# A tile loop turned into a ring of 16 steps, with each hop between engines in a step of its own

## The chip, the cores and the metric

The kernel runs on one core of a Trainium2 chip. The metric is the device time of one launch in microseconds (us); lower is better. A core has five engines that work side by side, each from an instruction stream of its own, in order: TensorE (PE, matmuls and transposes into PSUM banks; PEld is its weight load), VectorE (DVE), ScalarE (ACT), GpSimd (POOL) and SyncE (SP, which here only starts DMAs). They meet at semaphores. An instruction that waits holds up all that stands behind it on its engine.

## The reference, cut to what matters

1024 tokens of 256 features (32 sequences of 32) go through three residual blocks:

```python
x = x + xattn(layernorm(x), ctx)   # 16 heads, 257 context rows of 64 per sequence, low-rank weights
x = x + attn(layernorm(x))         # 16 heads of 128, self-attention within 32 tokens, mxfp4 weights and biases
x = x + ffn(layernorm(x))          # router over 64 experts, top 8, capacity 128; silu(gate) * up, down
```

In the third block a token's slot in an expert is its rank among the tokens that chose that expert, counted over the tokens in order; tokens past slot 127 are dropped.

## The kernel before, in words

The tokens are cut into T = 8 tiles of 128 (four sequences each). The program has three stages: the weights of the first block are multiplied together ("fold"), then the tile loop, then the 64 experts.

In the tile loop each tile passes two pipelines. The first (X, tile i) is the cross-attention: 16 rows (4 sequences times 4 groups of heads). A row is `score_row` on PE (L1188, L1189), `max_row` on DVE (L830), `exp_row` on ACT (L609), `transpose_row` on PE (L1196), `copy_row` on ACT (L617) and `sum_row` on PE (L1207); every four rows DVE's `normalise` (L836 to L840) ends a sequence. Beside the rows stand the units of the list `XS`: `kt0` to `kt3` (the keys of a sequence, L1166, split in a high part by ACT and a low part by DVE, L592, L820), `cT0` to `cT3` (L1171), and, for the next tile, `hT` (L1155), `qa` and `qb` (the queries of 8 head pairs, L1161, L588, L824); `out` is the output product (L1175) that DVE's `x_out` adds to the tokens (L847). The second pipeline (S, tile j = i - 1, with parts for m = j - 1) is the self-attention and the routing, the list `SS`: `hT`, `q0` to `q3`, `k0` to `k3` (L1142 to L1144, drained by DVE in L867), `sc` (L1234, softmax L872 to L859), `v0` to `v3` (drained by ACT, L630), `pv0` to `pv3` (L1244, split by ACT L634 and DVE L883); and for tile m `wo0` to `wo3`, `rT`, `log`, `pos` with DVE's `self_out` (L928), `chosen` (L903 to L907), `weigh`, `place` (L919 to L921). Both lists go through two PSUM banks each, a unit to one bank in turn, so unit n can start only when unit n - 2 has been drained. DVE's `norm_root` and `norm_apply` (end L811) make the layernorms; `next_h1` (L946) makes the one of the next tile.

The order of work is written out by hand. Every engine runs the same function `tile(i, j, m)` of STEPS = 21 steps: steps 0 to 15 each hold one row, and the tables `X_AT` and `BEHIND` say at which step a unit stands, on all engines. Rows and the units of X come ahead of the units of S in a step. The last five steps have no score row: `qb` stands at step 18, `cT3` and `kt0` at 19, `out` at 20, and only then does the next call of `tile` begin, whose row 0 waits for `qb` and `kt0`. A unit's matmuls, its drain by ACT and its drain by DVE are all in the same step.

POOL makes the rotated context (`rope_products` L456 to L461, `rope_sums` L471), the last of the 257 rows (`last_rows` L479), the low parts of the weights in tile 0 (L503), and scatters the rows of tile m to the experts with 8 indirect DMAs (`scatter`, L488) once `slot` is known; `scattered` then frees `h3`. SP's queue loads the context of tile i when the sums of tile i - 1 are made. The S pipeline starts with tile 0 when the X pipeline is at tile 1; after the last tile come two calls without X. The experts start when the last scatter has landed.

Of the kernel before, what the change touches and what calls it, by code (L numbers as in the profile page):

```python
# [12 lines left out]
P = 128  # L13
# [17 lines left out]
XS = ["kt1", "kt2", "cT0", "kt3", "cT1", "cT2", "hT", "qa", "qb", "cT3", "kt0", "out"]  # L31
XSPLIT = ["kt1", "kt2", "kt3", "qa", "qb", "kt0"]
XNEXT = ("hT", "qa", "qb", "kt0")
# [4 lines left out]
SS = ["wo", "hT", "q0", "q1", "q2", "q3", "k0", "rT", "k1", "k2", "log", "k3", "sc", "v0", "pos", "v1", "v2", "v3",  # L38
# [28 lines left out]
def build(nc, x, ctx_in, Wq, kcq, kckv, Wqr, Wkr, Wo_x, codes, scales, bq, bk, bv, bo, rw, gup, dnp,  # L67
# [5 lines left out]
    with ctx:  # L73
# [189 lines left out]
        def xpos(name, i, more=1):  # L263
            n, i = XS.index(name), i if name in XNEXT else i + 1
            return n % 2, i * (len(XS) // 2) + n // 2 + more

# [7 lines left out]
        def high_count(name, i):  # L274
            return (i if name in XNEXT else i + 1) * len(XSPLIT) + XSPLIT.index(name) + 1

# [148 lines left out]
        def _(e):  # L425
# [24 lines left out]
            def rope_products(i):  # L450

                if not isinstance(i, int) or i > 0:
                    e.wait_ge(roped, i * (2 * BT))
# [29 lines left out]
            def scatter(j):  # L483

                e.wait_ge(slot_ready, j + 1)
                alone(e)
                for k in range(TOPK):
                    e.indirect_dma_start(XE[:, :], bass.IndirectOffsetOnAxis(ap=slot[:, k:k + 1], axis=0), h3[:, :], None,  # L488
                                         bounds_check=E * CAP - 1, oob_is_err=False).then_inc(scat, 16)
# [18 lines left out]
            def tile(i, m, last=False):  # L508
                if not last:
                    rope_products(i + 1)  # L510
                for b in range(BT):
                    last_rows(i, b)
                    if isinstance(i, int) and i == 0:
                        for r, u in TILE_PARTS.items():
                            if RB * b <= r < RB * (b + 1):
                                part_low(u)
                    if b == BT - 1 and m is not None:
                        scatter(m)
                    if not last:
                        rope_sums(i + 1, b)  # L520
                if m is not None:
                    scattered(m)

            tile(0, None)

            e.wait_ge(w_done, PARTS)
            e.memset(diag[:, :, :], 0.0).then_inc(zeroed, 1)
            tile(1, None)

            e.wait_ge(zero_out, 16 * (E // 8 + NY))  # L530
            for j in range(1, T - 2):
                tile(j + 1, j - 1)
            tile(T - 1, T - 3, last=True)
            for m in (T - 2, T - 1):
                scatter(m)
                scattered(m)
# [17 lines left out]
        def _(e):  # L554
# [44 lines left out]
            def exp_row(i, r):  # L599
                e.wait_ge(maxed, i * ROWS + r + 1)  # L600
                if r % RB == 0:

                    b = r // RB
                    if b >= 2:
                        e.wait_ge(on_ready, i * BT + b - 1)
                    elif not isinstance(i, int) or i > 0:
                        e.wait_ge(on_ready, i * BT + (b - 1))
# [4 lines left out]
            def copy_row(i, r):  # L612
                e.wait_ge(transposed, i * ROWS + r + 1)

                if r >= 2:
                    e.wait_ge(summed, i * ROWS + r - 1)
# [27 lines left out]
            def spread(j, q):  # L644

                e.wait_ge(sT_ready, j + 1)
# [3 lines left out]
            def tile(i, j, m, last=False):  # L650


                def uses(names):
                    for name in names:
                        t = m if name in BEFORE else j
                        if t is not None:
                            s_use(name, t)

                for r in range(STEPS):
                    if i is not None:  # L660
                        if 2 <= r <= ROWS + 1:
                            copy_row(i, r - 2)
                        if r < ROWS:
                            exp_row(i, r)
                        for name in X_AT.get(r, ()):
                            if name in XNEXT and not last:
                                x_use(name, i + 1)
                            elif name not in XNEXT and name != "out":
                                x_use(name, i)
                        if isinstance(i, int) and i == 0 and r in TILE_PARTS:  # L670
                            part_high(TILE_PARTS[r])
                    if j is not None and r in (13, 14):
                        for q in (0, 1) if r == 13 else (2, 3):
                            spread(j, q)
                    uses(BEHIND.get(r, ()))


            e.sem_inc(x_high, XSPLIT.index("qa"))
            for name in XNEXT:
                x_use(name, 0)  # L680

            tile(0, None, None)

            e.wait_ge(zeroed, 2)
            tile(1, 0, None)
            for j in range(1, T - 2):
                tile(j + 1, j, j - 1)
            tile(T - 1, T - 2, T - 3, last=True)
            tile(None, T - 1, T - 2)
            tile(None, None, T - 1)  # L690
# [19 lines left out]
        def _(e):  # L710
# [10 lines left out]
            def link(ins, which, base):  # L721

                done[which] = done.get(which, 0) + 1
                s, n = LINKS[which]
                ins.then_inc(s, 1)
                e.wait_ge(s, base * n + done[which])
# [20 lines left out]
            def all_stats(half):  # L747
# [8 lines left out]
                else:  # L756
                    e.wait_ge(n_link, 2 * T)
                    done["n"] = 2 * T
# [84 lines left out]
            def x_out(i):  # L843
# [5 lines left out]
                norm_stats(i, "s", i, st1, mv1)  # L849
# [89 lines left out]

            def self_out_norm(j):  # L940
# [9 lines left out]
            def tile(i, j, m, last=False):  # L950

                done.clear()

                def uses(names):
                    for name in names:
                        t = m if name in BEFORE else j
                        if t is not None and name[:2] != "wo":
                            s_use(name, t)

                for r in range(STEPS):  # L960
                    if i is not None:
                        if r < ROWS:
                            max_row(i, r)
                        if r % RB == 2 and r > RB:
                            normalise(i, r // RB - 1)
                        for name in X_AT.get(r, ()):
                            if name in XSPLIT and name not in XNEXT:
# [3 lines left out]
                        if r == 8 and not last:  # L971
                            next_h1(i + 1)
# [442 lines left out]
```

## Time and profile before

| | us |
|---|---|
| median of 3 runs | 780.78 |
| lowest, highest | 779.69, 794.77 |
| the profiled execution | 785.1 |
| its span | 783.3 |
| mean granted TensorE clock, share of full | 0.909 |

The profile is of one execution. Its span runs from the first to the last instruction; 1.8 us of the execution's time lie around it. Busy times are sums over instructions. A matmul's end is modelled, so after the last of a row of matmuls PE counts as busy for a moment more. A time in brackets in a timeline is how long the engine sat idle before the instruction, with what released it.

### The profile page before, as it was taken

To read this page: it belongs to the slowest core of one execution; us is meant where nothing else is said; L and a number is where in the kernel's file an instruction comes from. 1 tells how busy PE (TensorE), PEld (TensorE's weight loads), DVE (VectorE), ACT (ScalarE), POOL (GpSimd) and SP (SyncE) were. 2 spreads that over 40 slices of the span, in tenths; PEclk is the share of its full clock that TensorE was granted. 3 is DMA by queue.
4 is the path that set the end of the run, shared out by engine and by line. 5 is a ranking of instruction groups with operands and counts; after the bars stand their busy time and mean duration, and the time that the engine had idled before them with its cause. 6 is when DMAs were issued, how large, how long until landed. Compare 5 with 4: busy or idle time off the path is not lost.

```text
span 783.3 us, 16249 instructions
## 1 busy us (share of the span) xinstructions
PE 622.6 (79%) x6211; PEld 534.6 (68%) x6211; DVE 426.4 (54%) x1091; ACT 288.1 (37%) x798; POOL 294.7 (38%) x279
## 2 busy tenths in 40 slices
PE   6995677898999987898899798898874178898860
PEld 4884566797877876787787696796753067777750
DVE  1255485465676675676576577577653323333334
ACT  1123364337346345236236236246031033333320
POOL 3113299211214414313412412400303337777780
PEclk9975567999999999999999999999999579999995
DMA  7946993999001101100100200100101069999988
GB/s 200 293 140 156 237 251 84 294 338 300 6 2 53 38 3 54 35 3 34 55 3 18 72 2 2 69 2 2 66 2 51 28 167 284 301 301 296 303 168 275
DMA packets 98987, 97.61 MB, mean 125 GB/s; under 512 B 26238, under 2 KB 92848, under 8 KB 98912
## 3 DMA queue, kind: packets, MB, share of 16 engines
q1 hardware_dynamic: 86016, 78.21, 34.2%
q0 software_dynamic: 12288, 17.95, 10.5%
q8 instruction: 51, 0.84, 0.4%
q10 hardware_dynamic: 608, 0.42, 0.2%
q14 instruction: 24, 0.20, 0.1%
HBM read 62.32 MB, written 35.19 MB: 124 GB/s over the span
## 4 chain that ended last, share of the span: by engine, by line
PE 43%; DVE 20%; issue 13%; ACT 9%; POOL 6%; DMA 6%; another core or an unknown queue 2%; SPq 0%; POOLq 0%; DVEq 0%; PEldq 0%; ACTq 0%
POOL expert_sums L545 6%; PE bank L1161 5%; PE bank L1175 5%; PE bank L1142 5%; PE bank L1144 4%; PE bank L1143 4%; PE bank L1207 4%; DMA expert_sums<-Wh,etok 3%; PE bank L1244 3%; ACT pr L609 2%; DVE nmax L830 2%; PE bank L1196 2%; ACT diag L648 2%; ACT space L630 2%
## 5 line engine op out<-in xcount | busy, mean ns | idle before, releaser
L545 POOL DMA_INDIRECT expert_sums<-Wh,etok x64 | 98.8, 1544 | 37.8 <-issue 22.5
L609 ACT ACTIVATE pr<-bank,nmax 128x257 f32<-128x257 f32 x128 | 61.0, 477 | 101.4 <-DVE nmax L830 101.0
L1142 PE MATMUL bank<-space,Wh 128*128 128x128 f16 x512 | 88.3, 219 | 9.9 <-DVE X L928 7.1
L488 POOL DMA_INDIRECT expert_rows<-h,slot x64 | 62.7, 980 | 87.5 <-DVE slot L921 70.4
L1143 PE MATMUL bank<-space,Wh 128*128 128x128 f16 x512 | 88.2, 219 | 0.0
L1144 PE MATMUL bank<-space,Wl 128*128 128x128 f16 x512 | 88.2, 219 | 0.0
L1207 PE MATMUL bank<-Cr,pT 128*128 128x64 f32 x512 | 77.0, 276 | 9.4 <-DVE On L840 8.4
L471 POOL TENSOR_TENSOR Cr<-C,Ct 128x192 f32<-128x192 f32 x64 | 41.7, 675 | 104.9 <-PE bank L1207 104.8
L1207 PEld LDWEIGHTS bank<-Cr,pT 128*128 128x128 f32 x512 | 72.4, 204 | 12.4 <-issue 11.1
L830 DVE TENSOR_REDUCE nmax<-bank 128x1 f32<-128x257 f32 x128 | 53.3, 418 | 42.8 <-PE bank L1189 40.6
L479 POOL TENSOR_TENSOR On<-Cr,pr 128x256 f32<-128x256 f32 x32 | 20.7, 647 | 138.4 <-ACT pr L609 138.4
L1345 PE MATMUL bank<-Wh,ring 128*96 128x128 f32 x512 | 68.1, 277 | 0.0
L617 ACT COPY pT<-bank 128x256 f32<-128x256 f32 x128 | 47.6, 372 | 43.0 <-PE bank L1196 42.3
L1142 PE MATMUL bank<-Wh,space 128*128 128x256 f16 (+1 forms) x192 | 59.2, 309 | 4.8 <-ACT space L630 3.3
L867 DVE SCALAR_TENSOR_TENSOR space<-bank,bqk 128x512 f32<-128x512 f32 x64 | 43.5, 689 | 33.1 <-PE bank L1144 33.0
L1345 PEld LDWEIGHTS bank<-Wh,ring 128*96 128x96 f32 x512 | 60.9, 166 | 0.4 <-issue 0.3
L1196 PE MATMUL bank<-ident,pr 128*128 128x128 f32 x256 | 52.6, 289 | 10.5 <-ACT pT L617 10.5
L1142 PEld LDWEIGHTS bank<-space,Wh 128*128 128x128 f16 x512 | 51.1, 100 | 13.0 <-DVE X L928 8.2
L1143 PE MATMUL bank<-Wl,space 128*128 128x256 f16 (+1 forms) x192 | 59.1, 308 | 0.0
L1144 PE MATMUL bank<-Wh,space 128*128 128x256 f16 (+1 forms) x192 | 59.1, 308 | 0.0
L1354 PE MATMUL bank<-ring,Wh 96*128 96x256 f32 x128 | 43.4, 420 | 13.4 <-DVE Wh L1031 9.9
L1143 PEld LDWEIGHTS bank<-space,Wh 128*128 128x128 f16 x512 | 50.1, 98 | 0.1
(175 smaller groups left out, 1401.0 us busy)
## 6 DMA issues: line engine op xcount, KB each, us to landing
ring<-L_ffn_gate_up_proj_dram SPq DMA_DIRECT2D x64, 192.0 KB
expert_rows<-h SPq DMA_DIRECT2D x8, 1284.0 KB, 15.7
Wh<-expert_rows SPq DMA_DIRECT2D x64, 160.5 KB
ring<-L_ffn_down_proj_dram SPq DMA_DIRECT2D x64, 96.0 KB
expert_sums<-h SPq DMA_DIRECT2D x4, 1152.0 KB, 13.4
C<-ctx_dram SPq DMA_DIRECT2D x24, 128.0 KB, 3.3
Wl<-expert_sums SPq DMA_DIRECT2D x3, 1024.0 KB, 6.9
space<-L_xattn_Wo_dram SPq DMA_DIRECT2D x8, 256.0 KB, 4.8
```

The costliest lines, as they stand in the source:

```text
L488: e.indirect_dma_start(XE[:, :], bass.IndirectOffsetOnAxis(ap=slot[:, k:k + 1], axis=0), h3[:, :], None, bounds_check=E * CAP - 1, oob_is_ ...
L545: e.indirect_dma_start(Y[n % NY][:, :], bass.IndirectOffsetOnAxis(ap=etok[:, n % 4:n % 4 + 1], axis=0), ye[:, n % 4], None, bounds_check=Y ...
L609: e.activation(pr[:, s, :], bank[r % 2][:, 0:NL], ACT.Exp, bias=nmax[:, s:s + 1], accum_out=rsum[:, s:s + 1]).then_inc(expd, 1)
L617: e.copy(pT[:, r % 2], bank[2][:, 0:2 * P].rearrange("p (c t) -> p c t", c=2)).then_inc(pt_ready, 1)
L830: e.tensor_reduce(nmax[:, s:s + 1], bank[r % 2][:, 0:NL], AX.X, ALU.max, negate=True).then_inc(maxed, 1)
L867: e.scalar_tensor_tensor((qS, kS)[w][:, 4 * g:4 * g + 4, :], src[:, :].rearrange("p (h t) -> p h t", h=4), 1.0 / WS, bqk[:, w, 4 * g:4 * g ...
L1142: e.matmul(dst, ah, bh, start=first and n == 0, stop=False)
L1143: e.matmul(dst, ah, bl, start=False, stop=False)
L1144: ins = e.matmul(dst, al, bh, start=False, stop=last and n == len(terms) - 1)
L1196: ins = e.transpose(bank[2][:, c * P:(c + 1) * P], pr[:, r % (2 * RB), c * P:(c + 1) * P], ident[:, :])
L1207: ins = e.matmul(bank[3][:, o:o + DC], pT[:, r % 2, c, :], Cr[:, b, c, 0, :], start=c == 0, stop=c == 1)
L1345: ins = e.matmul(bank[2 + n % 2][0:I, half * P:(half + 1) * P], gu[:, n, c, half * I:(half + 1) * I], xeT[:, n % 2, c, :], start=c == 0, s ...
```

## The change

All engines now run one ring: `step(g, t)` for n = 16 g + t, without a pause between tiles. A tile's rows stand at steps 0 to 15 of turn g, its last transposes and sums at steps 0 to 2 of the next turn, `cT3` at step 3, `out` at step 4; the S pipeline of a tile begins at step 5 and ends at step 3 of the turn after that. ACT and DVE have tables of their own, in which the drain by ACT and the drain by DVE often stand a step after the matmuls. Row 0 waits only for `qa`, row 2 for `qb`. DVE's `chosen` and `weigh` move behind the softmax, `pos` behind `v2`. POOL's work is put at steps, and the scatter is made in four pairs at steps 3 to 6.

```diff
-XS = ["kt1", "kt2", "cT0", "kt3", "cT1", "cT2", "hT", "qa", "qb", "cT3", "kt0", "out"]
+XS = ["kt1", "cT3", "out", "kt2", "cT0", "kt3", "cT1", "hT", "kt0", "qa", "qb", "cT2"]
+XTILE = {"cT3": -1, "out": -1, "hT": 1, "kt0": 1, "qa": 1, "qb": 1}
-X_AT = {2: ["kt1"], 6: ["kt2"], 7: ["cT0"], 10: ["kt3"], 11: ["cT1"], 15: ["cT2", "hT"], 16: ["qa"], 18: ["qb"],
-        19: ["cT3", "kt0"], 20: ["out"]}
+X_AT = {2: ["kt1"], 3: ["cT3"], 4: ["out"], 6: ["kt2"], 7: ["cT0"], 10: ["kt3"], 11: ["cT1"], 12: ["hT", "kt0"],
+        13: ["qa"], 15: ["qb", "cT2"]}
+X_LOW_AT = {3: ["kt1"], 7: ["kt2"], 11: ["kt3"], 13: ["kt0"], 14: ["qa"], 16: ["qb"]}
-BEHIND = {0: ["wo0"], 1: ["wo1"], 2: ["wo2"], 3: ["hT", "wo3"], 4: ["q0"], 5: ["q1"], 6: ["q2", "q3"], 7: ["k0", "rT"],
-          8: ["k1", "k2", "log"], 9: ["k3"], 10: ["sc"], 11: ["v0", "pos"], 12: ["v1"], 13: ["v2"], 14: ["v3"],
-          15: ["pv0"], 16: ["pv1"], 17: ["pv2"], 18: ["pv3"]}
+S_FIRST = 5
+S_AT = {5: ["wo0", "wo1"], 6: ["wo2"], 7: ["hT", "wo3"], 8: ["q0", "q1"], 9: ["q2", "q3"], 10: ["k0"],
+        11: ["rT", "k1", "k2"], 12: ["log", "k3"], 13: ["sc"], 14: ["v0"], 15: ["v1"], 0: ["v2"], 1: ["pos", "v3"],
+        2: ["pv0", "pv1"], 3: ["pv2", "pv3"]}
+ACT_S_AT = {7: ["hT"], 11: ["rT"], 13: ["log"], 14: ["sc", "v0"], 15: ["v1"], 0: ["v2"], 1: ["v3"], 2: ["pv0", "pv1"],
+            3: ["pv2", "pv3"]}
+DVE_S_AT = {7: ["hT"], 8: ["q0", "q1"], 9: ["q2", "q3"], 10: ["k0"], 11: ["k1", "k2"], 12: ["log", "k3"], 13: ["sc"],
+            1: ["pos"], 3: ["pv0", "pv1"], 4: ["pv2", "pv3"]}
-STEPS = ROWS + 5
+ALL_STEPS = ROWS * (T + 2) + 9
...
+            def step(g, t):
+                if t == 0 and 1 <= g <= T:
+                    last_rows(g - 1, 3)
+                if t == 3 and 1 <= g < T:
+                    rope_sums(g, 3)
+                if t == 4 and g < T:
+                    last_rows(g, 0)
+                if t in (3, 4, 5, 6) and 3 <= g < T + 3:
...
+                    scatter(g - 3, (2 * t - 6, 2 * t - 5))
+                if t == 6 and g + 1 < T:
+                    rope_products(g + 1)
+                if t in (7, 11, 15) and g + 1 < T:
+                    rope_sums(g + 1, t // 4 - 1)
+                if t in (8, 12) and g < T:
+                    last_rows(g, t // 4 - 1)
+                if t == 8 and 3 <= g < T + 3:
+                    scattered(g - 3)
...
+            def step(g, t):
+                n = ROWS * g + t
+                j, m = turn_of(g, t)
+                if j is not None and t == 5:
+                    x_out(j)
+                if g < T:
+                    max_row(g, t)
+                if t % RB == 2 and RB + 2 <= n and n - RB - 2 < T * ROWS:
+                    normalise(*divmod((n - RB - 2) // RB, BT))
...
+                if j is not None and t == 5:
+                    norm_stats(j, "s", j, st1, mv1)
+                    norm_root("s", j, mv1, rs1)
+                if j is not None and t == 6:
+                    norm_apply(h2, j, "s", j, mv1, rs1, h2_ready)
+                if m is not None and t == 8:
+                    self_out(m)
+                if m is not None and t == 9:
+                    norm_root("r", m, mv2, rs2)
+                if m is not None and t == 10:
...
+                    self_out_norm(m)
...
+                if j is not None and t == 15:
+                    softmax_sum(j)
+                    softmax_end(j)
+                if m is not None and t == 0:
+                    chosen(m)
+                if m is not None and t == 1:
+                    weigh(m)
+                if m is not None and t == 2:
+                    place(m)
+                if t == 11 and g + 1 < T:
+                    next_h1(g + 1)
...
-                if r == 0:
-                    wait_pos(e, xd, xpos("qb", i))
+                if r in (0, 2):
+                    wait_pos(e, xd, xpos("qb" if r else "qa", i))
...
-                    e.wait_ge(on_ready, i * BT + b)
+                    e.wait_ge(x_link, 2 * (i * BT + b) - 1)
```

The first `step` is POOL's, the second DVE's; in DVE's the units of `DVE_S_AT` stand between `self_out_norm` and `softmax_sum`. ACT's has `copy_row`, `exp_row`, the units of `X_AT`, two of the four `spread` (L648, the softmax laid out as diagonal blocks) at steps 0 and 1 each, then the units of `ACT_S_AT`. PE's has `score_row`, the transposes of the row two steps back, the sums of the row three back, the units of `X_AT`, then those of `S_AT`. The last hunk lets the sums of a new sequence start after the first of `normalise`'s three instructions, not the third.

## Rows read from the trace of the kernel before

**Rows 1.** The span in 40 slices of 19.6 us, in tenths.

```profile
PE   6995677898999987898899798898874178898860
...
PEclk9975567999999999999999999999999579999995
```

**Rows 2.** Busy time by stretches: us; PE, PEld, DVE, ACT, POOL busy; clock; DMA; GB/s.

```profile
145.60:200.60 55.00, 51.32 (x627) 45.43 (x626) 32.33 (x74) 26.26 (x75) 12.82 (x18) 1.00 0.91 294
200.60:258.00 57.40, 52.90 (x646) 46.77 (x644) 38.91 (x104) 27.42 (x79) 17.24 (x21) 1.00 0.07 25
258.00:318.20 60.20, 52.33 (x621) 45.21 (x620) 39.55 (x104) 27.14 (x79) 19.01 (x23) 0.97 0.12 35
...
379.70:441.20 61.50, 53.64 (x634) 46.78 (x632) 40.54 (x103) 27.22 (x79) 19.08 (x23) 0.97 0.09 30
...
503.30:555.00 51.70, 46.90 (x593) 41.16 (x591) 34.33 (x97) 24.53 (x73) 7.59 (x10) 1.00 0.04 14
...
555.00:631.40 76.40, 36.42 (x490) 29.21 (x487) 33.31 (x97) 10.09 (x22) 18.29 (x19) 0.82 0.11 36
```

**Rows 3.** Waits of PE from 379.7 to 441.2 us: total, times, longest.

```profile
PE bank L1166 <- DVE qspace L824: 2.5, 1, 2.5
PE bank L1207 <- DVE On L840: 1.3, 1, 1.3
PE bank L1142 <- DVE X L928: 1.3, 1, 1.3
PE bank L1220 <- DVE h L811: 1.1, 1, 1.1
PE bank L1175 <- ACT cT L597: 0.7, 1, 0.7
```

**Rows 4.** Timeline of PE: start, us, instruction, idle before.

```profile
251.92 0.55 PE L1166 MATMUL bank<-ident,Cr 128*128 128x128 f32 x3 [1.57 <-DVE qspace L824]
252.32 3.69 PE L1175 MATMUL bank<-N,cT 128*128 128x256 f32 x16
...
415.86 0.27 PE L1188 MATMUL bank<-KTh,qspace 128*128 128x257 f16 x1
...
417.99 0.27 PE L1188 MATMUL bank<-KTh,qspace 128*128 128x257 f16 x1
...
433.98 0.55 PE L1166 MATMUL bank<-ident,Cr 128*128 128x128 f32 x3 [2.49 <-DVE qspace L824]
435.25 5.38 PE L1175 MATMUL bank<-N,cT 128*128 128x256 f32 x16 [0.72 <-ACT cT L597]
```

**Rows 5.** Groups of DVE from 379.7 to 441.2 us: busy us, mean ns, idle before.

```profile
L830 DVE TENSOR_REDUCE nmax<-bank 128x1 f32<-128x257 f32 x17 | 7.1, 418 | 9.4 <-PE bank L1189 9.1
...
L824 DVE TENSOR_TENSOR qspace<-bank,qspace 64x512 f16<-64x512 f32 x4 | 2.8, 689 | 2.7 <-issue 1.9 <-ACT qspace L588 0.8
...
L907 DVE TENSOR_REDUCE mask<-space 128x64 bf16<-128x512 f32 x1 | 1.1, 1096 | 0.0
```

**Rows 6.** Groups of ACT in the same stretch.

```profile
L609 ACT ACTIVATE pr<-bank,nmax 128x257 f32<-128x257 f32 x16 | 7.6, 476 | 15.7 <-DVE nmax L830 15.6
...
L648 ACT COPY diag<-space 32x512 f32<-32x512 f32 x4 | 2.4, 612 | 0.1
L630 ACT ACTIVATE space<-bank 128x512 f32<-128x512 f32 x4 | 2.4, 602 | 0.3 <-PE bank L1144 0.3
```

**Rows 7.** Timeline of DVE after the last output product: one undisturbed layernorm.

```profile
554.98 0.42 DVE L847 TENSOR_TENSOR X<-X,bank 128x256 f32<-128x256 f32 x1 [4.24 <-issue]
...
558.59 0.41 DVE L811 TENSOR_SCALAR h<-X,mv,rs 128x256 f32<-128x256 f32 x1
```

**Rows 8.** The scatter's group of POOL from 379.7 to 441.2 us.

```profile
L488 POOL DMA_INDIRECT expert_rows<-h,slot x8 | 7.8, 978 | 5.6 <-DVE slot L921 3.5 <-issue 2.1
```

**Rows 9.** Timelines of DVE and of POOL at 323 us.

```profile
323.05 1.97 DVE L811 TENSOR_SCALAR h<-X,mv,rs 128x256 f32<-128x256 f32 x1
...
323.07 1.80 POOL L461 TENSOR_TENSOR C<-C,cosT 128x768 f32<-128x768 f32 x1
```

More of the change, by code:

```diff
@@ L506, in _ @@
                 part_low(u)
[L508 to L536, printed above, removed]
+            def step(g, t):
[6 more added lines that the diff above has]
+                if t in (3, 4, 5, 6) and 3 <= g < T + 3:
+                    if g == 3 and t == 3:
+                        e.wait_ge(zero_out, 16 * (E // 8 + NY))
+                    scatter(g - 3, (2 * t - 6, 2 * t - 5))
[7 more added lines that the diff above has]
+                    scattered(g - 3)
+                if g == 0 and t in TILE_PARTS:
+                    part_low(TILE_PARTS[t])
+                if g == 1 and t == 9:
+                    e.wait_ge(w_done, PARTS)
+                    e.memset(diag[:, :, :], 0.0).then_inc(zeroed, 1)
+            for n in range(ALL_STEPS):
+                step(n // ROWS, n % ROWS)
             def add_out(j, first):
@@ L648, in spread @@
                 e.copy(diag[qs, :, qs], sT[qs]).then_inc(diag_ready, 1)
[L650 to L675, printed above, removed]
@@ L678, in _ @@
[L678 to L690, printed above, removed]
+            def step(g, t):
+                row = row_of(ROWS * g + t - 2)
+                if row:
+                    copy_row(*row)
+                if g < T:
+                    exp_row(g, t)
+                for name in X_AT.get(t, ()):
+                    if name != "out" and 0 <= g + XTILE.get(name, 0) < T:
+                        x_use(name, g + XTILE.get(name, 0))
+                if g == 0 and t in TILE_PARTS:
+                    part_high(TILE_PARTS[t])
+                j, m = turn_of(g, t)
+                if j is not None and t in (0, 1):
+                    spread(j, 2 * t)
+                    spread(j, 2 * t + 1)
+                for name in ACT_S_AT.get(t, ()):
+                    if name in BEFORE and m is not None:
+                        s_use(name, m)
+                    elif name not in BEFORE and j is not None:
+                        s_use(name, j)
@@ L692, in expert_copy @@
+            e.sem_inc(x_high, XSPLIT.index("kt0"))
+            for name in XS:
+                if XTILE.get(name, 0) == 1:
+                    x_use(name, 0)
+            for n in range(ALL_STEPS):
+                step(n // ROWS, n % ROWS)
             def expert_copy(ex, n):
@@ L1011, in _ @@
             next_h1(0)
-            for name in ("qa", "qb", "kt0"):
-                x_low(name, 0)
-            tile(0, None, None)
-            tile(1, 0, None)
-            e.wait_ge(zero_out, 16 * (E // 8 + NY))
-            e.tensor_scalar(h3[:, D + E:ROW], h3[:, D + E:ROW], float(-(B * S + P)), None, ALU.add).then_inc(zeroed, 1)
-            e.wait_ge(zeroed, 3)
-            for j in range(1, T - 2):
-                tile(j + 1, j, j - 1)
-            tile(T - 1, T - 2, T - 3, last=True)
-            tile(None, T - 1, T - 2)
-            tile(None, None, T - 1)
+            for name in XSPLIT:
+                if XTILE.get(name, 0) == 1:
+                    x_low(name, 0)
+            for n in range(ALL_STEPS):
+                step(n // ROWS, n % ROWS)
+            assert all(done[which, i] == count for which, count in (("x", XLINKS), ("s", SLINKS), ("r", RLINKS))
+                       for i in range(T)), done
             def experts(j, first):
@@ L1333, in expert_t @@
+            for name in XS:
+                x_item(name, -1)
+            for n in range(ALL_STEPS):
+                step(n // ROWS, n % ROWS)
             def expert_t(j, n):
```

188 lines of the change are left out of this document (83 added, 105 removed).

## The prediction, made before the change was run

> **What bounds the kernel now.** I first read the page: the PE and clock lines in slices [rows 1]. Up to 145 us the clock sits at about half and the weights of the fold and of the second block stream in. From 145 to 555 us (slices 7 to 27) PE is nearly full at the full clock. Then come a thin stretch to 631 us and the experts, which this change leaves alone. So the place to look is the tile loop, and the question is what PE lacks there.
>
> Second, busy time cut at the moments when DVE adds the cross-attention's product (`x_out`, L847) [rows 2]. The seven stretches are 55.0, 57.4, 60.2, 61.5, 61.5, 62.1 and 51.7 us. In a full one (379.7 to 441.2) PE is busy 53.6 of 61.5 us, DVE 40.5, ACT 27.2, POOL 19.1, and the clock is 0.97. PE is the bound engine, with 7.9 us of idle time.
>
> Third, PE's waits in that stretch [rows 3]: 2.5 for the low part of `qb` and 0.7 for `cT` at the seam, 1.3 for `normalise`, 1.3 for `self_out`, 1.1 for the layernorm, 6.9 of the 7.9. Fourth, the seam itself [rows 4]: PE stops 2.49 us before `kt0`, then 0.72 us, and the 16 matmuls of `out` take 5.38 us. Three tiles earlier, behind a stop of 1.57, they took 3.69. That is the clock's lower level (1.2 in place of 2.4 GHz) after the stop, worth 1.7 us. It happens in four of the seven stretches. A tile without any stop would take 61.5 - 7.9 - 1.7 = 51.9 us.
>
> **The seam goes.** Removed per full tile: the stops of 2.5 and 0.7 and the 1.7 of the clock, 4.9 us. `qb` is now needed only by row 2 of the next turn, and its drain has steps 15 and 16; `kt0` stands at step 12, three steps ahead of its use; `out` at step 4 has rows, `wo0` and `wo1` around it. The stop of `normalise` (1.3) goes too: the sums of a sequence wait for its first instruction, ahead of the two others. That makes 6.2. The stops of 1.3 and 1.1 stay in kind, since `self_out` and `hT` still are one hop each; they are in the next part.
>
> **What is late next.** I lay out one turn. Beyond its units every PE step has a row. One row and one `v` unit take 2.13 us (415.86 to 417.99) [rows 4]; the mean step is 51.9 / 16 = 3.2 us. A DVE instruction of 512 columns takes 0.69 us, `max_row` 0.42, the mask 1.10 [rows 5]. An `exp_row` holds ACT 0.48 us and a further read of its accumulator, some 0.57 in all; a `spread` takes 0.61 and a `v` copy 0.60 [rows 6]. The stops of the new turn:
>
> - `pos` at step 1, the largest. It needs DVE's mask. From the end of `sc` DVE has, in order: two softmax steps (1.4), a max and `normalise` (1.5), the low part of `qa` (1.3), a max and the softmax's end (2.8), a max and the low part of `qb` (1.8), and `chosen` (0.2 + 0.7 + 1.1): 10.8 us. PE has in that time the rows of steps 14 to 1, `v0` to `v2`, `qb` and `cT2`: three times 2.13, one more row of 0.8 and about 2.1 for the rest, 9.3 us. Stop: 1.5. Before, `chosen` stood with `k3`, where DVE had time.
> - `pv2` at step 3. It needs the drain of `pv0`, which on DVE stands behind `place` (1.6, step 2) and the low part of `kt1`: 1.0.
> - `hT` of S at step 7: from `x_out` to the layernorm's end DVE needs 4.0 us with nothing between (554.98 to 559.00) [rows 7], here with two maxes and one `normalise` (2.1) and a wait for step 6, 7.1 in all; PE has 7.0 us of work in steps 5 to 7. Stop: 0.2.
> - `q0` at step 8, behind `self_out`: 0.4 (1.3 before: it stood behind more of DVE's waits for ACT).
> - `rT`, `k1`, `k2` at step 11: they wait for `self_out_norm`, for the drain of `k0` behind it, and for `rT`'s copy behind `exp_row`: 0.3, 0.4, 0.2.
> - `hT` of X at step 12: `next_h1` stands last in DVE's step 11, behind the drain of `k2`: 0.4.
> - `pv0` at step 2: ACT's copy of `v3` stands behind two of the `spread`: 0.25.
>
> Together 4.65. In the profile's counting each stop is 0.16 shorter, since PE counts as busy for 0.16 after its last matmul, so nine stops come to 3.2.
>
> **POOL and DVE together.** One mechanism speaks against the new places. At 323.05 `norm_apply`'s last instruction took 1.97 us, where it takes 0.41 alone [rows 7, 9]; it ended as POOL's L461 (1.80 us, from 323.07) did. DVE's instruction waited while POOL worked on SBUF. Before, this hit two of the full tiles. Now the eight scatters (0.98 each, 1.3 apart with the issue gaps [rows 8]) stand ahead of `rope_products` on POOL: from the slots at step 3 they run about 10.3 us, with `last_rows` between, so the products (L461 and two shorter instructions) fall on steps 5 to 7, where `normalise` and `norm_apply` stand and `hT` has no slack. I take 0.7 us a tile. The bounds: 0, when they miss each other, and 2.0, when both DVE instructions meet L461 for its 1.80 us. The Trainium skill's page GPSIMD Engine Reference, section Key points, says that GpSimd shares its SBUF interfaces with VectorE and contends with instructions in a 2-port mode or with two SBUF inputs. By that rule alone (L811 and L840 both fall under it) a collision would be the rule in every tile rather than in two, and the sum would carry the 2.0; the trace agrees on the kind, with its 1.97 against 0.41.
>
> For short stops that I can't see I add 0.7 (the three smallest of the tile now come to 7.9 - 6.9 = 1.0). A full turn: 51.9 + 3.2 + 0.7 + 0.7 = 56.5 us. Bounds of what the trace can't show, the sum of the new stops: 0 and, if each of `pos` and `pv2` waits 2 us longer and the clock falls once (1.7), 3.2 + 4 + 1.7 = 8.9, so 51.9 to 62.2 a turn. I take 56.5, since each of its terms is a sum of measured durations.
>
> **The sum.** Three turns against 61.5, 61.5 and 62.1: 5.0 + 5.0 + 5.6 = 15.6. The one against 60.2: 3.7. Against 57.4 (no clock loss there): 56.0, so 1.4. Against 55.0 (no part for tile m, so no `pos`): 53.0, so 2.0. The last, against 51.7 with 46.9 busy: 49.5, since fewer units cover the same hops, so 2.2. Up to the first `x_out` five rows of tile 1 are now done as well, in a stretch that the loads of the weights hold (DMA is behind it, not PE): 1.5 earlier, between 0 and 4. After the last `x_out` 76.4 us pass to the experts [rows 2], a chain of single hops with PE 36.4 busy. Its order is nearly the same; `chosen` leaves the way of the softmax (2.0) but `pos` now holds `v3`: 1.0 earlier, between 2 later and 3 earlier. The scatter in pairs costs nothing: POOL works 19.1 of 61.5 us, the last pair's end is behind by less than a step, and `scattered` at step 8 stands two steps ahead of its need (`h3` at step 10). In the last two turns POOL has nothing else. The expert stage is unchanged.
>
> Total 15.6 + 3.7 + 1.4 + 2.0 + 2.2 + 1.5 + 1.0 = 27.4. The profiled execution's 785.1 becomes 757.7 (span 755.9). The median of the runs shown stands 4.3 below the profiled execution; 780.8 - 27.4 gives **753** for the median.
>
> **The rivals.**
> - *The ring closes fully.* The stops I worked out overlap with each other (a delay at `pos` gives DVE time for `place`), and a turn takes near 51.9. Against the seven stretches: 9.6 + 9.6 + 10.2 + 8.3 + 5.5 + 3.7 + 4.8 = 51.7, with the two ends 54: 727. For it: DVE has 21 us free in a tile. Against: DVE's free time doesn't lie between `sc` and `pv`, where it is busy for some 17 us in a row. Chance 0.10.
> - *The seam moves.* The stop at `pos` grows beyond 2.4, so that the clock falls there as it did at 433.98. A turn: 56.5 + 1.5 + 1.7 = 59.7, which gives back 3.2 in five turns, 16 us: 769. For it: one slow link in DVE's long chain is enough, as `normalise` with POOL beside it. Against: a stop of 1.57 leaves `out` at 3.69 [rows 4], and `pos` has 1.5. Chance 0.18.
> - *Slower.* DVE's chain from `sc` to `pv3` becomes the ring. The mechanism is `place`, `chosen` and `pos` between the maxes: `max_row` of steps 1 to 3 comes late, so `exp_row`, so the scores two rows on, and `pv` as well. It decides once DVE's stretch from step 13 to 4 is over 5 us longer than I have it: then both stops pass 2.5 us, and the clock falls twice: 56.5 + 5 + 3.4 = 64.9, 3.4 to 7.5 worse than before in five turns (21 us in all), less some 3 of the 6.7 won at the ends: 798. Chance 0.07.
> - *The change doesn't do what it says*: `out` or row 0 still wait a whole hop at the turn (`cT3` is copied by ACT behind `exp_row` of step 3). Its cover is `pv2`, `pv3` and a row, over 2.5 us against 2.0. If it fails, 0.7 to 2 us a turn: about 760, inside my range, and I count it in.
>
> **How the numbers follow.** 0.65 for 753 (its own range 744 to 764, from turns of 55 to 58.5), 0.10 for 727, 0.18 for 769, 0.07 for 798. The range 737 to 773 leaves out the last and most of the first. Faster by over 2% means below 765.2 (2% is about what a measurement of this kernel can tell from no change): nearly all of the first case, the ring closing, and a little of the moved seam: 0.76. Within 2%: the rest of those, 0.17. Slower by over 2%: 0.07.
>
> **What would show it.** Stretches between `x_out`s of 55.5 to 57.5 us at a clock of 1.00, `out` at about 3.7 us in all of them, and no wait of PE for `qspace` L824 or `cT`. A wait of L1258 (`pos`) for the mask of 1 to 2 us, and one of L1244 for DVE L883 of about 1, each once a turn. POOL's L461 beside a long L811 or L840. Wrong would be: a clock of 0.97 in the full turns, a wait over 2.4 us at `pos`, DVE idle of less than 10 us a turn, or a stretch behind the last `x_out` that differs from 76 by more than 3.

## The result and the profile after

| | before | changed |
|---|---|---|
| median, us (20 runs each) | 786.51 | 780.06 |
| lowest, highest | 779.69, 795.37 | 765.58, 789.67 |
| the profiled execution | 785.1 | 783.59 |
| its span | 783.3 | 781.8 |
| mean granted clock | 0.909 | 0.894 |
| first `x_out` | 145.63 | 149.67 |
| last `x_out` | 554.98 | 553.24 |

The change makes the kernel 1.4% faster here: the ratio is 0.9858, with a 95% interval of 0.9815 to 0.9900. (On the second chip of the experiments no difference can be told: 0.9959, with 0.9868 to 1.0049.) The ratio compares undisturbed runs alone, so it isn't the quotient of the two medians. The forecast, 753 us within 737 to 773, was wrong: 27.4 us were promised, and some 6.5 (by the medians) to 11 (by the ratio) came.

The page after, the span in 40 slices of 19.5 us (those of before are [rows 1]):

```profile
PE   6999577898998899898988989899875088888850
...
PEclk9955657899999999999999999999998579999995
```

The tile loop still fills slices 7 to 27 and the clock line still reads 9, so the page doesn't tell why. The stretches between the `x_out`s do (L848 now; columns as in [rows 2]; the cut at 552.80 stands 0.4 us ahead of the last `x_out`, so the seventh stretch is really 48.0 us):

```profile
149.70:206.90 57.20, 52.32 (x627) 45.84 (x626) 31.84 (x72) 26.63 (x75) 15.66 (x19) 0.97 0.94 292
206.90:263.30 56.40, 51.60 (x634) 45.67 (x633) 39.71 (x103) 27.29 (x79) 12.67 (x18) 1.00 0.07 20
263.30:323.30 60.00, 53.40 (x634) 46.94 (x633) 40.50 (x102) 27.55 (x79) 18.85 (x24) 0.97 0.09 30
323.30:383.90 60.60, 54.79 (x634) 48.31 (x633) 40.56 (x102) 27.45 (x79) 18.71 (x23) 0.94 0.09 30
383.90:443.80 59.90, 53.40 (x635) 46.40 (x633) 40.31 (x102) 27.55 (x79) 18.72 (x23) 0.97 0.09 30
443.80:505.20 61.40, 54.82 (x634) 47.16 (x633) 40.42 (x102) 27.54 (x79) 18.68 (x23) 0.94 0.06 23
505.20:552.80 47.60, 44.35 (x567) 38.65 (x566) 32.62 (x90) 20.67 (x59) 9.08 (x10) 1.00 0.07 26
552.80:631.00 78.20, 40.03 (x506) 32.11 (x506) 33.66 (x97) 12.25 (x26) 19.42 (x20) 0.80 0.15 50
```

Two columns matter. The clock: the turn at 1.00 takes 56.4 us, where 56.0 was forecast; the four behind it have 0.97 or 0.94 and take about 60 to 61. PE's busy time: the same 634 instructions need 51.60 us at 1.00, 53.40 at 0.97 and 54.8 at 0.94, so one step of the clock column is 1.4 to 1.8 us. PE works longer on the same work; its idle time, 5.8 to 6.6 us in these four turns, is less than the 7.9 of before.

PE's waits in the turn from 323.3 to 383.9 (total, times, longest):

```profile
PE bank L1251 <- DVE mask L907: 1.9, 1, 1.9
PE bank L1213 <- DVE h L812: 1.7, 2, 1.2
PE bank L1163 <- DVE On L841: 1.1, 1, 1.1
PE bank L1237 <- DVE space L883: 0.6, 1, 0.6
PE bank L1147 <- DVE h L952: 0.4, 1, 0.4
```

Against [rows 3], the stops for `qspace` and for ACT's `cT` are gone, and nothing waits at the turn. The new first is `pos` (L1251, the mask), the second S's `hT` (L1213), the third one that I hadn't: a `cT` unit (L1163) that waits for `normalise`.

Where the clock falls is seen in short windows behind these stops, two behind the pair of L1163 and L1213 and two behind `pos`:

```profile
331.00:340.00 9.00, 7.58 (x77) 6.72 (x78) 5.33 (x17) 1.94 (x7) 1.70 (x3) 0.81 0.00 0
391.00:400.00 9.00, 6.82 (x87) 6.34 (x88) 6.57 (x19) 2.31 (x8) 2.13 (x4) 1.00 0.01 2
...
250.00:256.00 6.00, 5.59 (x45) 4.59 (x45) 5.36 (x16) 4.92 (x13) 1.14 (x2) 1.00 0.12 26
...
369.00:377.00 8.00, 7.16 (x45) 6.07 (x45) 6.41 (x18) 5.30 (x14) 1.19 (x3) 0.79 0.15 35
```

Each kind of stop appears once with the clock fallen (0.81, 0.79) and once without (1.00). Over the whole loop the clock fell behind two of the four pairs and behind four of the five stops at `pos`. It fell a seventh time in the first stretch, behind a pause of PE that the kernel before didn't have, in the middle of the small matmuls of the first `sc`; the profile names nothing that PE waited for there:

```profile
182.31 0.33 PE L1227 MATMUL bank<-space 128*32 128x32 f32 x16 [2.33 <-issue]
```

The timeline of PE shows one of each kind of stop (start, us, instruction, idle before):

```profile
331.23 0.41 PE L1163 MATMUL bank<-ident,On 128*128 128x128 f32 x2 [1.14 <-DVE On L841]
332.83 0.41 PE L1213 MATMUL bank<-ident,h 128*128 128x128 f32 x2 [1.20 <-DVE h L812]
...
333.30 0.27 PE L1136 MATMUL bank<-Wh,space 128*128 128x256 f16 x1
...
334.21 0.42 PE L1135 MATMUL bank<-Wl,space 128*128 128x256 f16 x1
...
336.13 0.91 PE L1200 MATMUL bank<-Cr,pT 128*128 128x64 f32 x4
...
369.75 0.19 PE L1251 MATMUL bank<-mask,before 128*128 128x64 bf16 x1 [1.91 <-DVE mask L907]
...
372.04 0.95 PE L1200 MATMUL bank<-Cr,pT 128*128 128x64 f32 x4
...
376.12 0.56 PE L1200 MATMUL bank<-Cr,pT 128*128 128x64 f32 x4
...
380.24 3.67 PE L1167 MATMUL bank<-N,cT 128*128 128x256 f32 x16
```

The same form of four sums takes 0.91 or 0.95 us behind a stop and 0.56 later, and a 256-column matmul 0.42 for 0.27: the lower level, 1.2 GHz. `out`, which took 5.38 at the seam [rows 4], takes 3.67. The fall has not gone with the seam; it has moved, and mostly to two places.

The third stop has its cause on POOL. Timelines of DVE and of POOL at 329 us:

```profile
328.37 0.42 DVE L831 TENSOR_REDUCE nmax<-bank 128x1 f32<-128x257 f32 x1 [2.44 <-PE bank L1182]
...
329.37 1.71 DVE L841 TENSOR_TENSOR On<-On,rinv 128x256 f32<-128x256 f32 x1
...
332.27 0.41 DVE L812 TENSOR_SCALAR h<-X,mv,rs 128x256 f32<-128x256 f32 x1
```

```profile
328.99 1.81 POOL L481 TENSOR_TENSOR C<-C,cosT 128x768 f32<-128x768 f32 x1
```

`normalise`'s last instruction took 1.71 us, alone 0.43, and ended 0.28 us after the last instruction of POOL's `rope_products`. This is the collision that the prediction named, on L841 and not on L812. The first row is a second finding: DVE sat idle for 2.44 us, waiting for the score of row 6, with the end of S's layernorm queued behind.

Outside the loop: from the last `x_out` to the end 228.6 us, before 228.3. The first `x_out` came 4.0 us later, though the tile work in front of it is not slower: `next_h1` of tile 0, which ends the fold, whose code is unchanged, starts 5.8 us later than before. In ten profiles of nearly the same front this first `x_out` lies anywhere between 137.0 and 149.7 us, and this is why the loop below is compared from the first to the last `x_out`: before 409.3, changed 403.6.

### The profile page after: what moved, and what is told of

It reads as the page before. It is cut to its first block, busy times and chain, and to the rows that moved or that the text cites. A ratio compares the mean times of both kernels' runs of the same rounds, so it can differ in the third digit from the quotient of the medians.

```text
span 781.8 us, 16320 instructions
## 1 busy us (share of the span) xinstructions
PE 633.0 (81%) x6211; PEld 542.4 (69%) x6211; DVE 427.2 (55%) x1091; ACT 289.7 (37%) x798; POOL 293.8 (38%) x279
## 4 chain that ended last, share of the span: by engine, by line
PE 43%; DVE 25%; issue 12%; POOL 8%; DMA 6%; another core or an unknown queue 2%; ACT 2%; SPq 0%; POOLq 0%; DVEq 0%; PEldq 0%; ACTq 0%
PE bank L1134 5%; PE bank L1136 5%; PE bank L1135 5%; POOL expert_sums L563 5%; DMA expert_sums<-Wh,etok 4%; PE bank L1167 3%; PE bank L1237 3%; PE bank L1200 3%; PE bank L1153 3%; DVE On L841 3%; DVE qspace L825 2%; PE bank L1123 2%; PE bank L1111 2%; PE bank L1182 2%
## 5 line engine op out<-in xcount | busy, mean ns | idle before, releaser
L491 POOL TENSOR_TENSOR Cr<-C,Ct 128x192 f32<-128x192 f32 x64 | 38.5, 624 | 169.5 <-PE bank L1200 165.2
L1200 PEld LDWEIGHTS bank<-Cr,pT 128*128 128x128 f32 x512 | 75.1, 211 | 0.8 <-issue 0.5
L1134 PE MATMUL bank<-Wh,space 128*128 128x256 f16 (+1 forms) x192 | 61.8, 322 | 2.7 <-issue 2.4
L1136 PE MATMUL bank<-Wh,space 128*128 128x256 f16 (+1 forms) x192 | 62.1, 323 | 0.0
L1135 PE MATMUL bank<-Wl,space 128*128 128x256 f16 (+1 forms) x192 | 61.9, 323 | 0.0
L1134 PEld LDWEIGHTS bank<-space,Wh 128*128 128x128 f16 x512 | 50.8, 99 | 6.7 <-DVE space L867 2.8
L1034 DVE CAST etok<-Wh 128x1 uint32<-128x1 f32 x64 | 9.8, 153 | 73.9 <-DMA expert_sums<-Wh,etok 55.7
```

Of the source, the lines that this page charges most:

```text
L1134: e.matmul(dst, ah, bh, start=first and n == 0, stop=False)
L1135: e.matmul(dst, ah, bl, start=False, stop=False)
L1136: ins = e.matmul(dst, al, bh, start=False, stop=last and n == len(terms) - 1)
L1200: ins = e.matmul(bank[3][:, o:o + DC], pT[:, r % 2, c, :], Cr[:, b, c, 0, :], start=c == 0, stop=c == 1)
```

## The experiments

The theory after the first reading: the hand-laid stops stand about where they were put, and what is missing is the clock, which falls behind the stop at `pos` and behind the pair of `cT` and `hT`, plus POOL's collision in front of that pair; take the stops away and the falls go with them. The rivals: DVE's chain, or the scatter in pairs, sets the pace of the ring, and PE's stops only show it. A full turn is one of the third to sixth stretches. Stops of an experiment are named by the changed kernel's lines; where POOL's code has grown, lines behind it are six higher (L1213 is L1219, L1251 is L1257, L841 is L847, L883 is L889).

| kernel | median (runs) | ratio to before, 95% | loop, us | falls in it |
|---|---|---|---|---|
| before, first set | 786.44 (7) | | | |
| `chosen` ahead of `sc` | 770.2 (4) | 0.9822 (0.9761 to 0.9882) | 396.6 | 5 |
| products later | 767.55 (4) | 0.9751 (0.9700 to 0.9801) | 394.5 | 5 |
| both | 756.8 (4) | 0.9643 (0.9601 to 0.9685) | 383.1 | 0 |
| scatter in one block | 773.96 (4) | 0.9851 (0.9793 to 0.9909) | 397.5 | 2 |
| before, second set | 777.31 (19) | | | |
| before with the early sums | 783.16 (10) | 0.9959 (0.9887 to 1.0031) | 405.8 | 4 |
| both, layernorm first | 745.26 (4) | 0.9597 (0.9496 to 0.9698) | 373.7 | 0 |
| products later, `v3` ahead of `pos` | 755.66 (4) | 0.9731 (0.9657 to 0.9805) | 385.3 | 1 |
| the changed kernel again | 780.71 (10) | 0.9959 (0.9868 to 1.0049) | 407.9 | 8 |

The two sets ran on two chips, each with its own runs of before, so medians are compared within a set only; in the second, before spread from 762.0 to 793.3 us. The loop, from the first to the last `x_out`, and the falls of the clock in it are of one profile each; in the first profiles they were 409.3 us with 4 falls (before) and 403.6 with 7 (changed). On the second chip the changed kernel can't be told from before. Against the changed kernel's 0.9858 (0.9815 to 0.9900), the ratios of "products later" and "both" are clearly lower, that of `chosen` ahead of `sc` is not; there the profile has to tell.

**`chosen` ahead of `sc`.** DVE makes the mask at step 13, not at step 0 of the next turn; nothing else.

```diff
+                if m is not None and t == 13:
+                    chosen(m)
...
-                if m is not None and t == 0:
-                    chosen(m)
```

> The changed kernel with DVE's chosen at step 13, ahead of the softmax's maximum, where DVE sat idle for 2.5 us waiting for sc; pos keeps its place. Theory (two stops a turn, each with a fall of the clock behind it): the wait of pos for the mask (1.9 us) and the half-clock stretch behind it (3.6 us long, so about 1.8 us) go. A full turn falls from 60.6 to 57, the clock of the turns is 0.97, the kernel gains 3 to 3.5 us in each of 6 turns, about 18 us. Rival A (DVE is the bound of the ring from sc to pv3, wherever chosen stands): the stop moves to pv0 or pv2, the turn stays within 1 us of 60. Rival B (the clock falls whatever the stops are): the stop goes, the clock stays at 0.94 to 0.97, the turn is 58.7.

Measured: 770.2 us; full turns of 60.0, 58.5, 58.5 and 58.9. PE's waits from 309.0 to 367.5:

```profile
PE bank L1213 <- DVE h L812: 1.7, 2, 1.2
PE bank L1163 <- DVE On L841: 1.1, 1, 1.1
PE bank L1237 <- DVE space L883: 0.8, 1, 0.8
PE bank L1134 <- ACT space L643: 0.7, 1, 0.7
```

The stop at `pos` is gone, the pair stands, and the clock of the turn is 0.97, one step up from 0.94. In this profile it falls behind each of the four pairs and nowhere else in the full turns; in the turn of 60.0 it stayed down about twice as long (0.58 over 7.2 us). I had expected 57, with this one fall already in it, so the miss of one and a half us is idle time: between two turns that I compare (60.6 and 58.5 us) PE's idle time falls from 5.8 to 5.0 us, not by the whole 1.9, since a stop of 0.7 for ACT's drain of a `v` unit (L643) is new.

**Products later.** POOL's `rope_products` and the first `rope_sums` wait until ACT has done row 8, so that they miss `normalise` and `norm_apply` of steps 6 and 7.

```diff
-                if t == 6 and g + 1 < T:
-                    rope_products(g + 1)
-                if t in (7, 11, 15) and g + 1 < T:
+                if t == 6 and g == 0:
+                    rope_products(1)
+                if t == 7 and g == 0:
+                    rope_sums(1, 0)
+                if t in (11, 15) and g + 1 < T:
...
+                if t == 9 and 1 <= g and g + 1 < T:
+                    e.wait_ge(expd, g * ROWS + 9)
+                    rope_products(g + 1)
+                    rope_sums(g + 1, 0)
```

> The changed kernel with POOL's rope_products held back until row 8 of the turn has had its exponential, away from DVE's normalise and norm_apply of step 6. Theory: DVE's L841 at step 6 takes 0.42 in place of 1.7 us, PE's stop for cT0 (1.1) goes and that for hT falls from 1.2 to about 1, the clock holds there; a turn falls by 1.3 us and 1.7 of the clock, to 57.6, in 5 turns 15 us. Rival (the layernorm chain alone sets hT, POOL only fills its time): hT's wait grows to 2.3 and nothing is won. Rival B as above: 1.3 us a turn, about 6 us.

Measured: 767.55 us. Two turns, from 319.0 to 377.7 and from 377.7 to 434.7:

```profile
319.00:377.66 58.66, 53.22 (x634) 46.52 (x633) 39.11 (x102) 27.54 (x79) 18.65 (x23) 0.97 0.10 31
...
377.66:434.66 57.00, 51.81 (x634) 45.73 (x633) 39.12 (x102) 27.36 (x79) 18.64 (x23) 1.00 0.10 32
```

and the waits of the second:

```profile
PE bank L1257 <- DVE mask L913: 1.9, 1, 1.9
PE bank L1219 <- DVE h L818: 1.5, 2, 1.0
PE bank L1243 <- DVE space L889: 0.7, 1, 0.7
```

The stop of the `cT` unit is gone (L847 takes 0.43 at 325.09, with POOL's products from 330.3 on), the wait for `hT` stays at 1.1 and didn't grow to the rival's 2.3, and no fall follows the lone `hT`. The full turns are 57.0 to 58.7 us and the loop is 9 us shorter than the changed kernel's, where I had expected 57.6 and 15: four of the five stops at `pos` still have a fall behind them. The two turns shown differ by 1.66 us, with the same stop of 1.9 at `pos` in both: in one the clock falls behind it, in the other it doesn't. That is the price of a fall: 1.4 us of PE's busy time, and a stop at `pv2` of 1.2 us in place of 0.7.

**Both.**

> Both edits together. Theory: they add, a full turn is 54 us with the clock at 1.00 and no stop over 1.2 us; about 30 us less than the changed kernel, 745 to 752. Rival A: 58 to 60 a turn. Rival B: clock still 0.97 or less, 57 a turn.

The edit is the two diffs together. Measured: 756.8 us, turns of 54.9 to 56.1, the clock 1.00 in all of them. That is 2 us a turn and 5 us in all above what I expected. One turn, and PE's waits in it:

```profile
307.02:362.88 55.86, 51.84 (x634) 45.77 (x633) 39.13 (x102) 27.47 (x79) 18.65 (x23) 1.00 0.10 32
```

```profile
PE bank L1219 <- DVE h L818: 1.6, 2, 1.1
PE bank L1243 <- DVE space L889: 0.8, 1, 0.8
PE bank L1140 <- ACT space L649: 0.7, 1, 0.7
```

Each edit alone leaves one place where the clock falls; together they leave none, and the kernel that the change was meant to be comes out: PE busy 51.84, the 51.9 of the prediction. Against the changed kernel's turn of 60.6, with two falls, a turn of 55.9 has 3.0 less of PE's busy time and 1.8 less of idle time. A pace set by DVE has no term for the first. The whole loop is 20.5 us shorter; seven falls at about 1.65 us are some 11.6 of it, an estimate, and the stops themselves the other 9. The pause in the first `sc` is still there (2.5 us), this time without a fall.

**Scatter in one block.** All eight indirect DMAs at step 3 instead of pairs at steps 3 to 6.

```diff
-                if t in (3, 4, 5, 6) and 3 <= g < T + 3:
+                if t == 3 and 3 <= g < T + 3:
...
-                    scatter(g - 3, (2 * t - 6, 2 * t - 5))
+                    scatter(g - 3, range(TOPK))
```

> The changed kernel with the scatter's eight DMAs in one block at step 3, nothing else. Theory: last_rows of the turn's first sequence then stands behind 10 us of scatter on POOL and ends at about step 5 or 6, so normalise and with it the layernorm of step 6 come later: 0 to 1.5 us a turn slower. If the pairs were themselves the cost (issue gaps, POOL late for rope_products), it is faster by 0.3 to 1 us a turn.

Measured: 773.96 us; its ratio to before, 0.9851, is that of the changed kernel in the first measurement, so the pairs cost and give nothing that can be told. In the turn from 320.5 to 378.9 the `cT` stop is 0.3 and not 1.1: POOL's L481 starts 1 us ahead of DVE's L841 instead of 0.4, so that L841 takes 1.1 us and not 1.7. The clock holds at 1.00 there, although `pos` waits 1.9 there. It fell behind two of the five stops at `pos`.

**Before with the early sums.** The last hunk of the change alone, on the kernel before.

```diff
-                if r % RB == 0:
+                if r % RB == 0 and i * BT + b >= 1:
...
-                    e.wait_ge(on_ready, i * BT + b)
+                    e.wait_ge(x_link, 2 * (i * BT + b) - 1)
```

> The kernel before with one part of the change alone: the sums of a new sequence wait for normalise's first instruction in place of its third. My prediction's term: PE's stop of 1.3 us for DVE On L840 goes in each full turn, so 1.3 us less in five turns, 6 us in all; the clock of the turns stays at 0.97, since the stop of 2.5 us at the seam is untouched. Rival: the sums run on and PE then waits at the next hop for the same DVE chain, within 2 us of before.

Measured: 783.16 us, no difference that can be told (the 6 us expected would lie within the interval too). The trace decides: the stop of the sums for `normalise` is 0.6 us in place of 1.3 [rows 3], and 3.3 us later the stop for ACT's copy (L1196, waiting for L617) is 0.6 where it was 0.2. So of the 1.3 a turn at which I had priced the hunk some 0.3 is won, and the rest comes back as a shorter stop and at the next hop, as the rival said; the loop of the profile is 3.5 us shorter, not 6. The seam stands, with stops of 2.4 us and a fall behind each of three. In the turn whose seam stops were 1.71 and 0.91 us there was no fall; before, 1.77 and 0.94 had one.

**`v3` ahead of `pos`.** On "products later": PE's `v3` stands in front of `pos` in step 1, so that it covers most of the wait for the mask. DVE's order is untouched. This tells apart whether the length of PE's stop or DVE's chain counts.

```diff
-        11: ["rT", "k1", "k2"], 12: ["log", "k3"], 13: ["sc"], 14: ["v0"], 15: ["v1"], 0: ["v2"], 1: ["pos", "v3"],
+        11: ["rT", "k1", "k2"], 12: ["log", "k3"], 13: ["sc"], 14: ["v0"], 15: ["v1"], 0: ["v2"], 1: ["v3", "pos"],
```

> e2 (products late, chosen still at step 0) with PE's pos behind v3 and not ahead of it; DVE's order is as in e2. Theory (the clock falls behind a stop near 1.9 us at the full turn's step 1, so the stop's length matters and not the sum of stops): the wait for the mask falls to about 0.6 us, v3 covers the rest, the clock of the turns is 1.00 and a turn 55.5 to 56.5, near e3. Rival (DVE's chain is the bound there): the time comes back at pv0 or pv2, which wait 1 us longer, and the turn stays at 57 to 58.7 with a clock of 0.97.

Measured: 755.66 us. One turn and its waits:

```profile
367.50:423.67 56.17, 51.72 (x634) 45.67 (x633) 38.73 (x102) 27.38 (x79) 18.75 (x24) 1.00 0.10 32
```

```profile
PE bank L1243 <- ACT space L649: 1.5, 1, 1.5
PE bank L1219 <- DVE h L818: 1.0, 2, 0.5
PE bank L1257 <- DVE mask L913: 0.6, 1, 0.6
```

`pos` waits 0.6, `pv0` now 1.5, no fall, and the turn is as long as with `chosen` early. DVE still makes the mask behind the softmax. But one of the five turns with these two stops does have a fall, which begins at 299.76, within the stop of 1.5 (297.25 is the end of the stop of 0.6):

```profile
253.94:313.01 59.07, 54.41 (x646) 48.31 (x645) 38.70 (x103) 27.40 (x79) 21.10 (x26) 0.97 0.12 39
```

(12 instructions of the next turn are counted in this one; the two together take 113.6 us.) So one undivided stop of 1.9 us had a fall behind it in four of five turns of "products later", two of 0.6 and 1.5 in one of five. The loop is 9.2 us shorter, of which four falls fewer are some 6.6 (an estimate, at 1.65 each) and the rest idle time. That DVE's chain alone sets the pace doesn't fit this, though part of the wait did come back at `pv0`, as the rival said. This rests on one profile of each: the ratios to before on the two chips, 0.9751 and 0.9731, can't be told apart.

**Layernorm first.** On "both": `norm_apply` of S moves ahead of `max_row` in step 6, where DVE had idled 2.4 us for row 6, and `next_h1` a step forward.

```diff
+                if j is not None and t == 6:
+                    norm_apply(h2, j, "s", j, mv1, rs1, h2_ready)
                 if g < T:
                     max_row(g, t)
...
-                if j is not None and t == 6:
-                    norm_apply(h2, j, "s", j, mv1, rs1, h2_ready)
...
-                if t == 11 and g + 1 < T:
+                if t == 10 and g + 1 < T:
                     next_h1(g + 1)
```

> Both edits of e3, and further DVE's norm_apply of step 6 ahead of max_row, where DVE sat idle 2.4 us for row 6's scores, and next_h1 a step earlier, at the end of step 10. If the layernorm's stop (1.1) and that of next_h1 (0.4) are order alone, both go and a full turn falls from 55.9 to 54.4, the kernel by some 8 us against e3, to 748. If row 6's maximum is what the turn hangs on, nothing is won: max_row comes 1.6 us later, then exp and the scores of row 8.

Measured: 745.26 us, full turns of 54.2 to 54.5, as expected, and no fall. PE's waits in the turn from 303.3 to 357.5:

```profile
PE bank L1243 <- DVE space L889: 0.8, 1, 0.8
PE bank L1140 <- ACT space L649: 0.7, 1, 0.7
PE bank L1219 <- DVE h L818: 0.5, 1, 0.5
```

The layernorm's `h` is ready before its maximum now, and the stop of 1.1 is gone. This kernel is 4.0% under before, with an interval of 3.0 to 5.0%. It can't be told by time from "both", which ran on the other chip at 3.6%; the loops of the profiles are 373.7 and 383.1 us.

**The changed kernel again.**

> The changed kernel itself once more, beside the others on this chip: 775 to 783 us, full turns of 60 to 61 us at a clock of 0.94 to 0.97 with the same stops (mask 1.9, layernorms 1.7, normalise 1.1).

Measured: 780.71 us. Full turns of 61.1 to 61.5, the waits as in the first profile's turn to 0.1 us but 1.2 for L1237. The clock falls behind all four pairs (behind the first for about twice as long, 0.57 over 7 us) and behind three of the five stops at `pos`; all four turns show 0.94. So a turn of the same code takes 60 or 61.5 us by how long the clock is down in it.

## Why the prediction was wrong

*What bounds the kernel*: PE, with its stops and the clock behind them. Right. PE's busy time without a fall was put at 51.9 and is 51.4 to 52.3 in the full turns at 1.00 that hold the same number of instructions, give or take two. (One reading was loose: the clock line of [rows 1] is at 9 for the first 40 us and at about half only from there to 145 us. Nothing hangs on it.)

*The seam goes*: right for the seam. No wait for `qspace` or ACT's `cT`, `out` at 3.67. The 1.3 for the early sums was too much: on the kernel before, the hunk won some 0.3 by the stops.

*The stops of the new turn*: their places were right, the sizes about so. `pos` 1.5 (less 0.16 in the profile's counting) was 1.91; `pv2` 1.0 was 0.6 to 1.2; `hT` of X 0.4 was 0.4; `q0` 0.4 was 0.2. One term was mis-sized: `hT` of S at 0.2 was 1.2, and stays 1.1 without the collision. I had counted the work in DVE's way (7.1) against PE's (7.0). But the maximum of row 6 stands ahead of `norm_apply`, and row 6 is scored late: in "both" `h` is ready 8.0 us after `x_out`. "Layernorm first" removes the term.

*POOL and DVE together*: the mechanism was right, the size too small. I took 0.7 a turn, between 0 and 2.0; it is 1.1 (the stop of L1163), in each of the four full turns, where before it hit two tiles. The page GPSIMD Engine Reference of the Trainium skill, section Key points, states the contention for this kind of instruction. Taken as a rule for every tile, the trace agrees with it by frequency; by size (one collision a turn, 1.3 us, for two) it takes some two thirds of that 2.0.

*The clock*: this is the step that failed. The sum puts a fall behind the new stops at nothing, and the rival *the seam moves* had the fall begin at a stop of 2.4, because a stop of 1.57 had left `out` at 3.69. The trace of before could have warned: at 372.24 a stop of only 1.77, with 0.94 behind it, was followed by an `out` of 5.38. I had counted that fall among the four and not looked at its stop. In the changed kernel the clock fell behind 1.91 alone in four of five cases and behind the pair (as 1.14 with 1.20 after it) in two of four. A clock of 0.97 in the full turns was the first of the signs of being wrong that I had named. The rival was right in kind, but that its 59.7 for a turn was nearly met (59.9 to 61.4) is partly luck: it took 1.5 us from a longer stop at `pos`, which didn't come, and one fall a turn, where two of the four full turns had two; the rest came from `hT` and POOL.

The account, from first to last `x_out`: forecast 24.9 less than before, measured 5.8, so 19.1 are missing. The falls, counted by the clock column (one in the first stretch, none in the second, then 1, 2, 1, 2, none): seven at about 1.65 us, 11.6. The four full turns, besides their falls, are 15.9 - 6 x 1.65 = 6.0 over the forecast, 1.5 each, which the collision's 0.4 and the 1.0 of `hT` nearly fill. The first stretch has 2.5 more than its fall explains, and the pause of 2.33 us inside its `sc` is nearly all of that. All eight profiles of kernels with the ring have this pause, 1.85 to 2.61 us, and neither of the two without it; the prediction had no term for it. The second is 0.4 over, the last 1.5 under.

*The ends*: 1.5 and 1.0 were promised. At the tail nothing came (228.6 against 228.3). At the front the promise can't be read, since the fold moves the first `x_out` by up to 12.6 us between profiles.

*The scatter in pairs costs nothing*: right, within what four runs can tell.

*The chances*: within 2% of before, which is what came, had 0.17, and *the seam moves* 0.18. With the 1.57 and the 1.77 side by side, a stop expected at 1.5, with a doubt of a few tenths, should have made the fall as likely as not, and the forecast should have moved towards that rival's 769.

What stays open: why the same stop is followed by a fall in one turn and not in the next, what PE waits for in the first `sc`, and what makes the fold's end vary, and with it the medians of before (786.4 and 777.3 in the two sets).

## What to carry to other kernels

When stops of a full PE are summed, each has two prices, its length and a chance of a clock fall behind it. Two short stops with work between them can be cheaper than one, so it can pay to put a unit that is ready into a long stop even where most of the wait comes back; but two stops close together can bring the clock down where one of them alone doesn't. Sort the stops of the trace before by length, each with the clock behind it, before you call a length free. And a schedule with hops in steps of their own moves work on every engine: ask for each two-input DVE instruction what POOL does beside it now, and for each short DVE instruction at the end of a chain whether it is queued behind one that waits for a later row.

## What the hardware showed

- The clock falls behind short stops, and not every time. Behind the 1.91 us stop at `pos` it fell in 4 of 5 turns of the changed kernel, 4 of 5 with the products later, 2 of 5 with the scatter in one block and 3 of 5 in the repeat. Behind the pair (1.0 to 1.4, then 1.2, 1.6 us apart) it fell 2 of 4 times, then 4 of 4 and 4 of 4. In six of these ten falls behind a pair the clock fell within the second stop. Behind a lone stop of 1.0 to 1.1 it fell in none of the full turns of "both" and of "products later"; behind a lone stop of 1.5 to 1.7 in none of nine cases in the two kernels without the ring, but behind one of 1.76; behind the pause of 1.85 to 2.61 in the first `sc` in four of eight.
- A fall of the clock costs 1.66 us where two turns differ in little else; PE's busy time grows by 1.4 to 1.8. Twice it stayed down for about twice as long, both times at a pair whose first stop was 1.4.
- A two-input DVE instruction of 0.43 us that starts beside POOL's product of 1.81 us takes 1.1 to 1.8 us and ends 0.28 us after it, in each of 16 meetings in four profiles. Beside POOL's `rope_sums` (0.59 us) the same instruction takes 0.75 to 0.85, before the change as well (0.67 to 0.85).
